# Layer 0 of a four-layer graph network on one Trainium2 core: block one-hots in smaller instructions, the clear of the sums on ScalarE, three reorderings

## The reference, cut to what matters

```python
h = node_features @ W_t
msgs = h[edge_col]
agg_sum = jax.ops.segment_sum(msgs, edge_row, num_segments=n)
deg = jax.ops.segment_sum(jnp.ones_like(edge_row, dtype=h.dtype), edge_row, num_segments=n)
agg = agg_sum * jnp.where(deg > 0, 1.0 / deg, 0.0)[:, None]
return jax.nn.relu(jnp.concatenate([node_features, agg], axis=-1) @ W_u + b_u)
```

## Time and profile before

| | |
|---|---|
| runs | 8705.8, 8714.9, 8717.0 us, median 8714.9 |
| profiled execution | 8707.9 us, span 8706.1 us, TensorE clock granted 0.837 |
| busy, share of the span | TensorE 71%, VectorE 62%, ScalarE 43%, POOL 72% |
| layer 0, gathers | 136 to 2379 us |
| layer 1, gathers | 2434 to 4254 us |
| layers 2 and 3, gathers | 4372 to 6459 us and 6499 to 8624 us |

### The profile page before, as it was taken

How to read it: one execution, slowest core, us unless ns; L and a number is a source line. 1 busy time by engine, 2 the same in 40 slices (tenths; PEclk the granted TensorE clock), 3 DMA queues, 4 the chain that set the end, 5 groups by cost and what they waited for, 6 DMA issues and landing times. The chain is left out here.

```text
span 8706.1 us, 153774 instructions
## 1 busy us (share of the span) xinstructions
PE 6202.1 (71%) x41943; PEld 5309.4 (61%) x41944; DVE 5376.6 (62%) x10966; ACT 3768.3 (43%) x8055; POOL 6245.2 (72%) x6523
## 2 busy tenths in 40 slices
PE   5788888888869999999634444444446777777776
PEld 2566666657769898999633333333336666666665
DVE  8898898888877888877722222222225555555554
ACT  5445355342052222222422222222236777777775
POOL 3677777777757766777477777777767777777774
PEclk7899999998789999999866666666668888888887
DMA  1122122121142222222222222222223443334432
GB/s 35 43 52 52 51 52 52 51 52 49 44 130 63 57 52 54 54 56 55 77 64 64 60 64 60 64 64 60 64 64 105 110 110 110 108 110 109 111 108 71
DMA packets 575365, 611.58 MB, mean 70 GB/s; under 512 B 114414, under 2 KB 472474, under 8 KB 574618
## 3 DMA queue, kind: packets, MB, share of 16 engines
q0 software_dynamic: 203776, 417.74, 18.9%
q1 hardware_dynamic: 294120, 145.77, 5.8%
q10 hardware_dynamic: 76722, 38.13, 1.5%
HBM read 562.68 MB, written 38.51 MB: 69 GB/s over the span
## 5 line engine op out<-in xcount | busy, mean ns | idle before, releaser
L2014 POOL DMA_INDIRECT M<-in_x,ixb x1664 | 1696.3, 1019 | 538.5 <-issue 530.0
L2195 PE MATMUL ps<-M,oh 128*128 x7056 | 1285.8, 349 | 1064.5 <-ACT M L2550 1034.1
L2061 POOL DMA_INDIRECT M<-t,ixb x1664 | 1615.7, 971 | 503.9 <-issue 498.1
L2195 PEld LDWEIGHTS ps<-M,oh 128*128 128x128 f32 x7056 | 1194.0, 253 | 1240.1 <-issue 1176.3
L2061 POOL DMA_INDIRECT M<-x,ixb x1664 | 1577.5, 948 | 503.9 <-issue 503.1
L2014 POOL DMA_INDIRECT M_any<-t,ixb x1376 | 1302.3, 946 | 501.1 <-issue 445.4
L1435 ACT ACTIVATE oht<-oneh,ot 128x128 f16<-128x128 f16 x3264 | 965.3, 387 | 979.6 <-DVE oneh L1411 979.6
L2213 DVE TENSOR_TENSOR acc<-acc,ps 128x1024 f32 x294 | 357.9, 1217 | 1587.5 <-PE ps L1776 1587.5
L1954 DVE TENSOR_TENSOR acc<-acc,ps 128x774 f32 (+1 forms) x988 | 942.7, 954 | 570.7 <-PE ps L1776 542.5
L2550 ACT ACTIVATE M<-M,wD 128x128 f32<-128x128 f32 x1664 | 517.1, 388 | 1488.2 <-DMA M<-x,ixb 1473.2
L1924 PEld LDWEIGHTS ps<-M,oh 128*128 128x128 f32 x5928 | 894.5, 209 | 266.0 <-issue 160.3
(11 more groups left out here) (306 smaller groups left out, 9256.1 us busy)
## 6 DMA issues: line engine op xcount, KB each, us to landing
er<-in_edge_attr SPq DMA_DIRECT2D x414, 256.0 KB
M<-in_x,ixb POOLq DMA_INDIRECT x1664
M<-x,ixb POOLq DMA_INDIRECT x1664
M<-t,ixb POOLq DMA_INDIRECT x1664
M_any<-t,ixb POOLq DMA_INDIRECT x1376
x<-lay SPq DMA_DIRECT2D x48, 256.0 KB, 2.4
part<-x ACTq DMA_DIRECT2D x48, 256.0 KB, 4.6
lay<-in_x SPq DMA_DIRECT2D x24, 256.0 KB, 3.9
```

Source lines behind the costliest of these rows:

```text
L2014: e.indirect_dma_start(M1[:, m1_slot(s, t), :] if layer else M[:, t % RING, 0:P], None, table[0:rows, :], bass.IndirectOffsetOnAxis(ap=ixb ...
L2061: e.indirect_dma_start(M2[:, t % RING, :], None, table[:, :], bass.IndirectOffsetOnAxis(ap=ixb[:, t:t + 1], axis=0)).then_inc(s_g[n % 16], 16)
L2195: ins = e.matmul(ps_flat[:, bass.ds(slot * P, P)], oh[:, j, :], tile_at(M2, tile, P), start=False, stop=False)
```

## The change

1. `ohh` is written by 16 instructions of two groups each in place of four of eight. Each is an operation of its own in the merged order. TensorE's counts still wait for the last instruction of their eight groups.
2. `shared` is 6 in place of 7 in the lead-in sorts: ScalarE scales six columns (12 products) and VectorE two (4 instructions).
3. ScalarE zeroes `acc` by a copy of a zero column, as its first instruction; POOL's memset is gone.
4. `places` for supertile 0 runs between the two degree periods; the instructions on degrees come straight after the copy of the totals; the eight instructions that prepare the `dst` tables come after the node parts. The counts that ScalarE and TensorE wait for follow (`V_DEG` 12 to 4, and 3 to 11 after the parts).

The degree matches (L1504) stay as they are.

```diff
--- before.py
+++ after.py
@@ -1271,12 +1271,13 @@
                         cur["pay"] = tv.at()
 
                     for q in {0: (0,), 1: (1, 2), 2: (3,)}.get(i, ()):
-                        ohh_at[q] = v(lambda: e.tensor_tensor(
-                            ohh[:, 8 * q:8 * q + 8, :, :],
-                            iota4[:, :, :].rearrange("p (a b) c -> p a b c", a=1).to_broadcast([P, 8, NB, 4]),
-                            khi[:, 32 * q:32 * q + 32].rearrange("p (g a c) -> p g a c", a=1, c=4).to_broadcast([P, 8, NB, 4]),
-                            ALU.is_equal), chain=q == 0)
-                        yield OP
+                        for g in range(8 * q, 8 * q + 8, 2):
+                            ohh_at[q] = v(lambda: e.tensor_tensor(
+                                ohh[:, g:g + 2, :, :],
+                                iota4[:, :, :].rearrange("p (a b) c -> p a b c", a=1).to_broadcast([P, 2, NB, 4]),
+                                khi[:, 4 * g:4 * g + 8].rearrange("p (g a c) -> p g a c", a=1, c=4).to_broadcast([P, 2, NB, 4]),
+                                ALU.is_equal), chain=g == 0)
+                            yield OP
 
                         def count_groups():
                             for g in range(8 * q, 8 * q + 8):
@@ -1413,7 +1414,7 @@
                             def scaled_column(k, w, pf):
                                 return lambda: e.tensor_scalar(oht[:, r, k, w * P:(w + 1) * P], iota128b[:, :], tile_f[:, h, k:k + 1],
                                                                pf[:, 8 * c + k:8 * c + k + 1], ALU.is_equal, ALU.mult)
-                            shared = 7 if s < 2 else 8
+                            shared = 6 if s < 2 else 8
                             for k in range(8):
                                 if k < shared:
                                     v(one_column(k), *([lane_at[c], *free] if k == 0 else []), chain=False)
@@ -2363,7 +2364,6 @@
                 stores_done(e, tal)
 
             def run_pool(e):
-                e.memset(acc_flat, 0.0).then_inc(s_z, 1)
                 tal = part_tallies()
                 for layer in range(4):
                     if layer < 2:
@@ -2404,10 +2404,21 @@
                     period(s, sort(e, "v", s + 2, tv, tp, ta))
                 e.sem_inc(s_srt, 1)
                 period(SUP - 2, degrees(e, "v", 0, HALF, tv, tp, ta))
+                tm = Tally(s_map)
+                e.wait_ge(s_v, tv.n)
+                places(e, tm, 0)
                 period(SUP - 1, degrees(e, "v", HALF, SUP, tv, tp, ta))
 
                 tp.inc()
                 v(lambda: e.tensor_copy(tot[:, :], ps[:, 7, 0:NB]), tp.at())
+                v(lambda: e.tensor_scalar(degm[:, :], degD[:, :], 0.5, None, ALU.is_gt))
+                v(lambda: e.tensor_scalar(degD[:, :], degD[:, :], 1.0, None, ALU.max))
+                v(lambda: e.reciprocal(degD[:, :], degD[:, :]))
+                e.wait_ge(s_a, 1)
+                v(lambda: e.tensor_tensor(degD[:, :], degD[:, :], degm[:, :], ALU.mult))
+                tal = part_tallies()
+                e.wait_ge(s_v, tv.n)
+                all_parts(e, "v", 0, tal)
                 v(lambda: e.tensor_tensor_scan(endp[:, :], ones_f[:, 0:NB], tot[:, :], 0.0, ALU.mult, ALU.add))
                 v(lambda: e.tensor_copy(endi[:, :], endp[:, :]))
                 v(lambda: e.tensor_scalar(endi[:, :], endi[:, :], 7, None, ALU.logical_shift_right))
@@ -2416,17 +2427,6 @@
                 v(lambda: e.tensor_tensor(endt[:, :], endt[:, :], ident[:, 0:NB], ALU.mult))
                 v(lambda: e.tensor_reduce(lcol[:, 0:1], endt[:, :], AX.X, ALU.add))
                 v(lambda: e.tensor_tensor(lcol[:, 0:1], lcol[:, 0:1], bigcol[:, :], ALU.add))
-                v(lambda: e.tensor_scalar(degm[:, :], degD[:, :], 0.5, None, ALU.is_gt))
-                v(lambda: e.tensor_scalar(degD[:, :], degD[:, :], 1.0, None, ALU.max))
-                v(lambda: e.reciprocal(degD[:, :], degD[:, :]))
-                e.wait_ge(s_a, 1)
-                v(lambda: e.tensor_tensor(degD[:, :], degD[:, :], degm[:, :], ALU.mult))
-                e.wait_ge(s_v, tv.n)
-                tm = Tally(s_map)
-                places(e, tm, 0)
-                tal = part_tallies()
-                e.wait_ge(s_v, tv.n)
-                all_parts(e, "v", 0, tal)
                 v(lambda: e.tensor_copy(ps[:, 6, 0:P], iota128[:, :]))
                 e.wait_ge(s_v, tv.n)
                 for u in range(2):
@@ -2463,7 +2463,7 @@
                 first_steps_d(e)
                 edge_dve(e, lambda m: group_dve_d(e, 3, regs, left, m, cleared), tick)
 
-            V_DEG = 12
+            V_DEG = 4
 
             def run_tensor(e, tv, tp):
                 ta = Tally(s_w)
@@ -2495,7 +2495,7 @@
                 all_parts(e, "p", 0, tal)
                 for t in tal:
                     wait(e, t[2].at())
-                tv.inc(3)
+                tv.inc(11)
                 pieces = dst_tables(e, "p", tv, tp, ta)
                 between = expand_pe(e)
                 at = [next(between)]
@@ -2527,6 +2527,7 @@
             def run_scalar(e, tv, tp):
                 ta = Tally(s_w)
                 ta.inc(W0)
+                e.activation(acc_flat, zwin[:, 0:1].to_broadcast([P, NB * W1C]), ACT.Copy).then_inc(s_z, 1)
                 e.wait_ge(s_wgt, NLD)
                 sorted_all(e, "a", tv, tp, ta, lambda s, gen: drain(gen))
                 tv.inc(V_DEG)
```

## The result

The changed kernel takes 8679.07 us (median of 6 runs, 8675.4 to 8686.78) against 8713.85 us (6 runs, 8705.77 to 8717.04) for the kernel before on the same chip: ratio 0.9961, interval 0.995 to 0.9972, or -34.8 us. The forecast was 8684 and -31. The execution that was profiled is the slowest of the six, 8686.78 us with a span of 8685.0; where it lost time is told under "From layer 1 on". Points and rows of a trace are from one profiled execution of each kernel.

What follows compares the result with a forecast made beforehand. VectorE's adds bound layer 0's first stretch, POOL's gathers the second. VectorE's terms summed to -27.9 us at layer 0's end, with POOL ahead at -32.7; the turn's -3.1 made -31: 8684 against 8714.9, range 8664 to 8704.

Steps and rivals of the forecast that it cites:

- What bounds the layer: Layer 0: VectorE's adds set the pace in the first stretch, POOL's gathers in the second; both limits must fall.
- The clear: Start of lead-in: POOL's memset holds VectorE's first instruction; clearing on ScalarE gives -10.2 us, ScalarE's 13.4 us hidden.
- The split: Lead-in sorts: ScalarE six columns, VectorE two; about -0.5 us per sort, -1.0 for both, bounds -3 and +1 each.
- The pieces on POOL: Merged sorts: shorter one-hots let waiting gathers in sooner; -2.2 us per sort, -22 over ten sorts, bounds 0 and -30.
- Rival A: POOL stays the limit, gathers not let in between pieces; relief 0 to 8 us, time 8693 to 8701; chance 0.18.
- The pieces on VectorE: Merged sorts: twelve more one-hot instructions cost VectorE +0.25 us per sort after idle time, +2.8 over eleven.
- rival D: Each small one-hot pays for the port; slower by +17 to +33 us, 8732 to 8748; chance 0.04.
- Supertiles 8 to 10: Last three supertiles before the degree periods: waits for gathers vanish once POOL leads again, -13.7 us.
- Degree periods and places: End of layer 0: TensorE's 11.3 us wait for arrivals goes; places between the periods stop VectorE, +5.0 us.
- rival B: VectorE isn't the limit at layer 0's end: places hide, split gives 3 us a sort; -41, 8674; chance 0.09.
- The turn to layer 1: Seam after layer 0: second turn on TensorE 5.3 us earlier, x load late next; prelude +2.2, net -3.1 us.
- the prelude: Eight instructions preparing the `dst` tables, moved behind the node parts before layer 1's first match batch; said to cost +2.2 us.

Runs made afterwards that it cites:

- iota_sbuf32: no_pieces with the one-hot's bf16 block-number table replaced by 32-bit values read from SBUF; one run, 8782.29 us against 8729.96 for the kernel before.
- iota_psum: no_pieces with the one-hot's bf16 block-number table replaced by 32-bit values read from PSUM; one run, 8761.25 us against 8729.96 for the kernel before.
- clear_only: Kernel before with only the clear of the sums moved to ScalarE; 9.4 us faster in the median than the kernel before (8714.0 us).
- no_pieces: Changed kernel with the one-hots back in four big instructions per sort; 8694.88 us against 8679.07 for the changed kernel.
- pieces_only: Kernel before with only the block one-hots cut into 16 instructions; 13.4 us faster than the kernel before (8714.0 us).
- share7: Changed kernel with the lead-in split left at 7:1, ScalarE scaling seven of eight columns; 8678.46 us against 8679.07 for the changed kernel.
- seam_back2: Changed kernel with places, prelude and degree instructions in their old order after the last add; ratio 0.9966 to the kernel before (8724.21 us on that chip).
- light4: Changed kernel with one-hots in 8 instructions per sort and places in layer 0's last six units; 8681.93 us, ratio 0.995 to the kernel before.

## Why the prediction was right, term by term

The stages of all traces but those of the slow chip and of `iota_sbuf32` and `iota_psum`, in us, show what repeats and how far executions scatter:

```
first sum to sums of supertile 8   big one-hots 1290.1 1289.2 1287.3     quarters 1294.0 1294.7 1293.4 1295.5   halves 1288.3
supertile 8 to 11                  big one-hots  498.2  499.9  497.3     quarters  484.2  487.3  487.0  485.4   halves  483.8
supertile 11 to last sum           big one-hots  359.6  357.1  357.3     quarters  350.1  350.5  350.4  352.3   halves  350.5
last sum to 65th gather            old seam      151.5  151.4  151.1  150.6     new seam  145.2  145.3  144.6  145.1
big: before, clear_only, no_pieces. quarters: after, pieces_only, share7, seam_back2. halves: light4.
old seam: before, clear_only, pieces_only, seam_back2. new seam: after, no_pieces, share7, light4.
```

Big one-hots and quarters, and the old and the new seam, stand apart in every row. Within a group the traces differ by 1 to 3 us, so a term of that size or less is not shown by one difference.

**What bounds the layer.** Right: VectorE's pace up to supertile 8, POOL's from there. `pieces_only` shows both: later at supertile 8 (+4.7), earlier at 11 (-6.2).

**The clear.** -10.2 forecast, -10.24 at the first instruction, -11.1 at the first sum. ScalarE's write was put at 13.4 us and took 10.74; hidden either way.

**The split.** -1.0 forecast for two sorts; the wait for TensorE at the sort's end fell from 9.93 us to 5.81, but only 0.4 us arrive at the first sum. Too small to be shown, within its bounds.

**The pieces on POOL.** Of the two ways it could go, the first was right: an end every 0.49 us lets POOL in. The size was low: -22 forecast over ten sorts, -29 in `pieces_only`, -30.6 in the changed kernel (gather 1408, less the earlier start). The sum allowed for three gathers in ten held over several pieces, as beside degree matches the earlier trace rows. Of 68 gathers beside pieces two were, 4.6 us in all. In the trace the stretch of gathers beside one-hots falls from 47.1 to 17.4 us: over 11 sorts 4.3 us each before and 1.6 after, where the forecast had 3.5 to 4.3 and 2.0, and took 2.2 out of the 1.5 to 2.3 that this leaves. Beside the lane and degree matches the stretch is smaller too (23.6 for 28.4, 37.4 for 44.7), but this is scatter: `pieces_only` has 28.8 and 42.0, `share7` 27.9 and 48.3. Rival A needed a relief of 0 to 8 us and is refuted.

**The pieces on VectorE.** Mis-sized: 0.25 us per sort forecast, 0.5 measured in the changed kernel (+3.9 over eight supertiles, -11.3 to -7.4), 0.6 in `pieces_only`, 0.8 against `no_pieces` (1294.0 - 1287.3 = 6.7 over eight). By the means of the table it is 0.7 (5.5 over eight), of the 1.0 that the 12 more instructions add. The idle time that was to take it up did so only in part. Halves cost nothing that can be seen (1288.3). Of rival D the direction was right and the price wrong: pieces stand 0.49 us apart as worked out, so none pays for the port.

**Supertiles 8 to 10.** -13.7 forecast, less 0.7 for the pieces, -14.0 measured (-7.4 to -21.4). At the first add of a supertile, POOL has started 18 gathers more than the supertiles before it hold at supertile 8 and 16 at 11 in the kernel before, 37 and 32 in the changed one.

**Degree periods and places.** -11.3 + 5.0 = -6.3 forecast, -9.5 measured. `pieces_only`, which moves nothing, gains 9.1 there, so the wait was worth 9 (7 by the means of the table) and the places cost nothing: with them between the periods 350.1 and 350.4, without them 350.5 and 352.3. This step of the forecast failed: "they stop VectorE while TensorE can run two groups ahead: +5.0". The bound at 0 was the right end, and rival B's "the places hide" came true while its 3 us a sort did not; the row with the 3.87 us wait would have said so. TensorE's wait for tiles is gone. The adds' waits in the two periods (us in total, times, longest) were, in the kernel before from 2033 to 2393 us,

```profile
DVE acc L1954 <- PE ps L1776: 33.6, 28, 9.7
```

and are, in the changed one from 2012 to 2362 us,

```profile
DVE acc L1955 <- PE ps L1777: 19.1, 26, 2.1
```

The 14.5 us less are about the 9.5 gained and the 5.8 of the places, which now lie in such waits. `pieces_only`, with no places there, has 23.6 us of them: 10.0 less than before for its 9.1.

**The turn to layer 1.** -5.3 forecast to the first part. Against the earlier trace rows:

```profile
2361.98 0.96 DVE L1955 TENSOR_TENSOR acc<-acc,ps 128x774 f32 x1 [0.41 <-PE ps L1777]
...
2365.61 2.59 SPq L1632 DMA_DIRECT2D lay<-in_x  x5
...
2365.92 0.17 DVE L1638 TENSOR_SCALAR lay<-acc 128x4 f32<-128x4 f32 x1
...
2368.82 1.94 PE L1608 MATMUL ps<-ident,lay 128*128 128x128 f32 x8 [6.68 <-DMA lay<-in_x]
...
2375.27 0.69 DVE L1653 TENSOR_TENSOR lay<-ps,bias 128x512 f32<-128x512 f32 x1 [5.46 <-PE ps L1650]
```

The load is late next, as said: TensorE turns x and the scaled rows in one go when x is there. L1653 stands at 2375.27 for 2411.85, -36.6, of which -30.9 came with the last sum: -5.7. Then the prelude, costed at +2.2, vanished:

```profile
2496.75 1.82 DVE L1937 TENSOR_TENSOR oh<-ps,relS 128x768 f32<-128x768 f32 x2
...
2498.65 0.43 ACTq L1836 DMA_DIRECT2D xw<-t  x1
2499.13 1.54 ACT L1847 ACTIVATE ps<-zwin 128x768 f32<-128x768 bf16 x2 [3.19 <-issue]
...
2507.19 0.94 POOL L2015 DMA_INDIRECT M_any<-t,ixb  x1 [28.80 <-issue]
```

VectorE's batch has shifted by 35.1 us (2531.81 to 2496.75), so the prelude does delay it by 2.2 of 37.3. But TensorE needs ScalarE's clear of the banks too, and that ends later (2499.13 + 1.54) than the batch (2498.57); it has shifted by the full 37.3 (2536.39 to 2499.13). The seam gives -6.4 instead of -3.1.

**The sum.** Four terms were off: pieces on VectorE 2 us too low, degree wait 2 too high, places 5 and prelude 2 too dear, 3 us together. The 65th gather came 6 us earlier than said; the other 3 are differences of 1 us and less in several stages, within the scatter. The median gain came out 4 us larger. The forecast's cause and size hold. That -31 is this close is in part luck, since errors of 4 us one way lie against 7 the other way; that 8684 lies so near the profiled 8686.78 is luck, by the next paragraph.

**From layer 1 on.** Through layer 2 the shift stays (-37.1). In layer 3 of this execution it falls to -22.1, because gathers there took 980 ns on average against 971 before. This differs from one execution to the next with the same instructions: from the last gather of layer 2 to the last of layer 3 are 2165.3 us in the kernel before, 2180.3 in the changed one, 2169.0 in `clear_only`, 2189.2 in `light4`. The median of runs, -34.8, agrees with the -37 of the trace before that layer.

## What to carry to other kernels

In these traces a VectorE instruction with two inputs in SBUF stopped indirect gathers for as long as it ran (up to 3.2 us more than the 0.94 alone), and one with an input in PSUM didn't: cut it short where POOL is the limit, or keep one input in PSUM. Cut it only as far as the gathers need, since VectorE paid 0.7 us per sort for quarters and nothing to be seen for halves, which served the gathers about as well. Before an insertion is priced, look for the wait that stands at that very place, on the same engine and on the one that joins it: both terms that went wrong by their whole size, places and prelude, lay in such waits. And compare two profiled executions at a point before the untouched stages, whose own scatter (15 us between these two, 24 among all) is as large as half of the effect.

## What was not expected of the hardware

A ScalarE write of 128x12642 f32 took 10.74 us, as fast as POOL's memset of the same (10.63 us), and from the 813 ns of 768 columns 13.4 had been expected. One of the chips ran every kernel at some 11260 us instead of 8700, with stops of up to 15.3 us; its cause stays open. The degree matches in halves, the one experiment on the rest of the stretched gathers, ran only there, so whether shorter degree matches pay isn't known.
